# Cross-attention on one core: half-tile scores in two PSUM banks, a five-bank ring, and two of four mask copies moved from VectorE to transfers

## The reference

```python
qp = (q @ Wq.T + bq).reshape(b, t_q, h, d // h).transpose(0, 2, 1, 3)   # q = layernorm(x)
kp = (k @ Wk.T + bk)...; vp = (v @ Wv.T + bv)...                        # k = v = ctx_1024
scores = jnp.einsum('bhqd,bhkd->bhqk', qp, kp) / jnp.sqrt(jnp.float32(d))
scores = jnp.where((attention_mask == 1)[:, None], -jnp.inf, scores)
attn = jax.nn.softmax(scores, axis=-1)
out = jnp.einsum('bhqk,bhkd->bhqd', attn, vp)                           # x = x + out
```

## Time and profile before

| | |
|---|---|
| Median of 3 runs | 2255.85 us (2254.08 to 2257.64) |
| The profiled execution, its span | 2242.05 us, 2240.1 us |
| First stage | 31 periods, about 120 to 1557 us of the span |
| PE, DVE, ACT, POOL busy | 83%, 71%, 47%, 57% of the span |
| DMA engines' share in the periods | 0.50 |

### The profile page before, as it was taken

How to read it: one execution, slowest core, us unless ns; L and a number is a source line. 1 busy time by engine, 2 the same in 40 slices (tenths; PEclk the granted TensorE clock), 3 DMA queues, 4 the chain that set the end, 5 groups by cost and what they waited for, 6 DMA issues and landing times. The chain is left out here.

```text
span 2240.1 us, 62734 instructions
## 1 busy us (share of the span) xinstructions
PE 1865.6 (83%) x24523; PEld 1272.5 (57%) x24523; DVE 1583.0 (71%) x3092; ACT 1053.8 (47%) x1399; POOL 1284.5 (57%) x618
## 2 busy tenths in 40 slices
PE   2688888889888898888988888888778787499996
PEld 1255555555555565555655555565335566388885
DVE  3588787778777787877877777788667776544442
ACT  2255555556555565555655555554354442133332
POOL 3356767667776677766777657675345432144442
PEclk9699999999999999999999999999785655699998
DMA  3445544455444554445544455443253324377774
GB/s 107 117 98 134 112 104 106 102 122 122 104 105 105 135 107 104 104 102 125 120 102 107 101 129 115 99 107 65 85 207 105 130 79 145 122 213 225 238 218 133
DMA packets 172384, 277.73 MB, mean 124 GB/s; under 512 B 66676, under 2 KB 140212, under 8 KB 171843
## 3 DMA queue, kind: packets, MB, share of 16 engines
q1 hardware_dynamic: 163300, 261.77, 45.9%
q0 software_dynamic: 8832, 12.06, 2.8%
HBM read 163.02 MB, written 31.98 MB: 87 GB/s over the span
## 5 line engine op out<-in xcount | busy, mean ns | idle before, releaser
L451 DVE CUSTOM_DVE_ANT_0 junk<-ring,mbias 128x898 bf16<-128x898 f32 (+1 forms) x512 | 523.6, 1023 | 208.6 <-issue 206.7
L361 POOL TENSOR_TENSOR p_sum<-p_sum,pT 128x1024 f32<-128x1024 f32 x256 | 657.1, 2567 | 12.5 <-ACT pT L571 0.6
L571 ACT ACTIVATE pT<-score,lift 128x1024 f32<-128x1024 f32 (+1 forms) x416 | 456.9, 1111 | 66.7 <-PE score L678 58.0
L342 POOL TENSOR_TENSOR cp<-cx,cp 128x768 f16<-128x768 f32 (+1 forms) x128 | 277.9, 2172 | 120.0 <-ACT cp L530 120.0
L644 PE MATMUL ring<-wvp,cp 128*128 128x256 f16 (+1 forms) x2496 | 317.0, 277 | 9.2 <-DVE mx L451 8.2
L578 ACT ACTIVATE v<-ring 128x512 f32<-128x512 f32 (+1 forms) x224 | 126.9, 566 | 413.5 <-PE ring L644 411.4
L358 POOL TENSOR_TENSOR p_sum<-pT 128x1024 f32<-128x1024 f32 x32 | 75.5, 2359 | 388.5 <-ACT pT L571 388.5
L678 PE MATMUL score<-qst,kst 128*128 128x64 f16 x6656 | 271.8, 196 | 17.0 <-issue 11.3
L678 PEld LDWEIGHTS score<-qst,kst 128*128 128x128 f16 x6656 | 239.3, 101 | 81.4 <-issue 48.0
L479 DVE COPY kst<-mbias 64x6144 f16<-64x6144 f16 (+1 forms) x128 | 280.6, 2192 | 4.0
L644 PEld LDWEIGHTS ring<-wvp,cp 128*128 128x128 f16 (+1 forms) x2496 | 231.3, 100 | 77.4 <-issue 29.4
(11 more groups left out here) (222 smaller groups left out, 2474.1 us busy)
## 6 DMA issues: line engine op xcount, KB each, us to landing
cx<-in_ctxT SPq DMA_DIRECT2D x32, 1601.0 KB, 7.4
w1p<-wsp SPq DMA_DIRECT2D x23, 1408.0 KB, 8.5
kst<-kh SPq DMA_DIRECT2D x512, 52.1 KB, 2.3
msk<-in_mask SPq DMA_DIRECT2D x64, 400.2 KB, 9.3
kst<-kh SPq DMA_DIRECT2D x512, 48.0 KB, 2.2
wsp<-w_parts SPq DMA_DIRECT2D x24, 704.0 KB, 3.7
w2p<-wsp SPq DMA_DIRECT2D x23, 640.0 KB
kst<-kl SPq DMA_DIRECT2D x256, 52.1 KB, 2.3
```

What stands on the lines that cost most here:

```text
L342: pool.tensor_tensor(cp[:, j, 1, :, chunk(n)], cx[:, :, chunk(n)], cp[:, j, 0, :, chunk(n)], ALU.subtract).then_inc(cl_ready, 1)
L361: pool.tensor_tensor(p_sum[:], p_sum[:], pT[:, u], ALU.add).then_inc(added, 1)
L451: dve.tensor_tensor_reduce(junk[:, n % 2, :, 0:MPAIR[half]], ring[:, 0:2, 0:MPAIR[half]], mbias[:, j, MS[2 * half]:MS[2 * half] + 2 * MPAI ...
L571: act.activation(pT[0:n, u], scored, ACT.Exp, bias=lift[0:n, 0:1], scale=SSCALE).then_inc(exp_done, 1)
```

## The change

Scores. A step S or E is now half a tile (8 of 16 heads, one bank), so there are 26 of each in a block; `scored` has 2 banks, and step s waits for E(s-2). The ring has 5 banks; a maxima unit takes banks 0 and 1 or 2 and 3 in turn, and T takes ring banks 0 and 1. The order of the units within a half changes (TURNS).

Shift. SH has two operations (a maximum, then a clip of 128x8), and SPR, the copy of 1x1024 out of PSUM, moves from DVE to ACT.

Mask. Copies 0 and 3 are transfers from SP now, from `mbias` to `kst`, 1024 rows each (64 partitions x 16 heads; 768 and 898 bytes). Copies 1 and 2 stay on DVE, each with its own semaphore.

Orders. All five strings are new. On SP the order goes from CX QS ST0 QR ST1 to MD3 QR CX QS MD0 ST0 ST1. On POOL the four CL come after all A. The rest of the kernel is as it was.

```diff
-PE_ORDER = steps("K0 S0 K1 K2 O S1 M0 K3 S2 M1 S3 K4 M2 W0 M3 W1 W2 S4 M4 K5 S5 W3 M5 S6 K6 M6 S7 S8 W4 M7 K7 M8 W5 W6 M9 S9 W7 S10 M10 "
-                 "V0 W8 M11 V1 W9 M12 V2 S11 M13 S12 V3 M14 W10 W11 M15 V4 W12 V5 T V6")
-POOL_ORDER = steps("A2 CL0 A3 A4 A5 QB A6 A7 CL1 A8 CL2 A9 A10 CL3")
-DVE_ORDER = steps("N MA3 KL0 KL1 KL2 R X0 KL3 X1 X2 KL4 X3 MA0 X4 KL5 X5 X6 KL6 X7 X8 KL7 X9 X10 MP X11 X12 X13 X14 MA2 X15 SH MA1 SPR")
-SP_ORDER = steps("CX QS ST0 QR ST1")
+PE_ORDER = steps("S0 K0 S1 K1 S2 K2 O S3 S4 M0 K3 S5 K4 M1 S6 S7 W0 W1 S8 M2 M3 S9 K5 M4 S10 W2 W3 S11 M5 S12 K6 S13 S14 W4 W5 S15 M6 M7  "
+                 "S16 K7 W6 S17 S18 M8 M9 V0 S19 S20 M10 W7 W8 W9 M11 S21 S22 V1 S23 S24 W10 M12 M13 S25 V2 W11 M14 M15 W12 V3 V4 T V5  "
+                 "V6")
+ACT_ORDER = steps("E0 KH0 E1 KH1 E2 E3 E4 KH2 E5 KH3 E6 KH4 E7 E8 E9 E10 KH5 E11 E12 KH6 E13 E14 E15 E16 KH7 CH0 E17 E18 E19 E20 VH0 CH1  "
+                  "E21 E22 VH1 E23 E24 E25 VH2 CH2 CH3 VH3 VH4 SPR VH5 VH6")
+POOL_ORDER = steps("QB A2 A3 A4 A5 A6 A7 A8 A9 A10 CL0 CL1 CL2 CL3")
+DVE_ORDER = steps("N KL0 KL1 R X0 KL2 X1 KL3 KL4 X2 X3 X4 KL5 X5 KL6 X6 X7 KL7 X8 X9 X10 X11 MA2 X12 X13 X14 X15 SH MP MA1")
+SP_ORDER = steps("MD3 QR CX QS MD0 ST0 ST1")
...
+            scored = c1.enter_context(nc.psum_tensor("scored", [P, 2, 512], F32))
+            ring = c1.enter_context(nc.psum_tensor("key_ring", [P, 5, 512], F32))
...
+                    def lay_mask(b, j, c):
+
+                        after(sp, st_done, HT * b + (2 * GT * (c + 1) - HT if c < KC - 1 else 0))
+                        if c == 0 and not has_later(b - 1):
+                            sp.wait_ge(mask_ready, 2 * b + 2)
+                        sp.dma_start(kst[MASK_AT:P, :, chunk(c)],
+                                     mbias[MASK_AT:P, j, MS[c]:MS[c] + KWIDTH[c]].bitcast(F16).unsqueeze(1).to_broadcast([S, H, KWIDTH[c]])).then_inc(laid[c], 16)
...
-                        dve.tensor_reduce(m8[:], mx[:], AX.X, ALU.max).then_inc(m8_done, 1)
+                        dve.tensor_reduce(top_m[:], mx[:], AX.X, ALU.max).then_inc(m_all, 1)
+                        dve.wait_ge(m_all, b + 1)
+                        dve.tensor_scalar(m8[:], top_m[:], MOST_SHIFT * SHIFT, -MOST_SHIFT * SHIFT, ALU.min, ALU.max).then_inc(m8_done, 1)
...
-                        after(pe, exp_done, b * KT + (kt - 1))
-                        for h in range(H):
+                        after(pe, exp_done, b * HT + (step - 1))
+                        for h in range(PAIRS * half, PAIRS * half + PAIRS):
...
+                        act.activation(pT[0:n, u, HALF * half:HALF * half + HALF], scored[0:n, half, :], ACT.Exp, bias=lift[0:n, 0:1],
+                                       scale=SSCALE).then_inc(exp_done, 1)
```

More of the change, by code:

```diff
@@ L271, in chunk, with unit @@
                 return slice(KS[n], KS[n] + KWIDTH[n])
+            def unit(n):
+                half, at = divmod(n, PAIRS)
+                return half, at // 4, TURNS[at % 4]
             def strip(r, c):
@@ L470, in prepare_mask @@
                         after(dve, m_read, MUNITS * (b - 1))
-                        after(dve, laid, KC * (b - 1))
+                        for c in (0, KC - 1):
+                            after(dve, laid[c], 16 * (b - 1))
                         dve.tensor_scalar(mbias[:, j, 0:MS[2] + KWIDTH[2]], msk[:, 0:KS[3]], 1, -MASKED, ALU.is_equal, ALU.mult).then_inc(mask_ready, 1)
@@ L494, in period @@
                                 shift(nb)
[L495 to L499, removed]
+                            elif kind == "MA" and do_b:
                                 lay_mask(nb, nj, n)
@@ L559, in keep_kh, with exponentiate, spread_shift @@
                         act.activation(kh[:, t, chunk(c)], ring[:, BANK["K", k], 0:KWIDTH[c]], ACT.Identity, bias=bks[:, c % 2, t:t + 1]).then_inc(kh_kept, 1)
[L561 to L571, removed]
+                    def exponentiate(b, j, step):
+                        kt, half = divmod(step, 2)
+                        n, u = KROWS[kt], (KT * j + kt) % SLOTS
+                        act.wait_ge(st_done, b * HT + (step + 1))
+                        if half == 0:
+                            held = weights_before(j, kt)
+                            after(act, pv_done, b * KT + (held + 1))
+                            if held % KT in SUMMED:
+                                after(act, added, b * ADDS + (max(SUMMED.index(held % KT), 1) - (ADDS if held < 0 else 0)))
+                        act.activation(pT[0:n, u, HALF * half:HALF * half + HALF], scored[0:n, half, :], ACT.Exp, bias=lift[0:n, 0:1],
+                                       scale=SSCALE).then_inc(exp_done, 1)
+                    def spread_shift(b, j):
+                        act.wait_ge(mt_done, b + 1)
+                        at = BANK["T", 0]
+                        act.activation(qst[0:1, j].rearrange("o h q -> o (h q)"), ring[0:1, at:at + 2].rearrange("o s k -> o (s k)"),
+                                       ACT.Copy).then_inc(qaug_ready, 1)
                     def keep_v(b, j, u):
@@ L590, in period @@
                                 high_context(b + 2, j, n)
+                            elif kind == "SPR" and do_b:
+                                spread_shift(b + 1, 1 - j)
                     periods(act, period)
@@ L624, in ring_free @@
                                 after(pe, v_kept, (b - lap) * VU + at + 1)
+                            elif held == "T":
+                                after(pe, qaug_ready, (b - lap) + 1)
                     def project_k(b, j, k):
```

85 lines of the change are left out of this document (47 added, 38 removed), and 3 rows, old and new, of the table BANK.

## The result

The changed kernel took 2393.45 us (median of 4 runs, 2390.50 to 2396.63), the kernel before 2256.74 us beside it: ratio 1.0607, 95% interval 1.0588 to 1.0626. It is 6.1% slower. The forecast was 2327 us, slower, with a range of 2215 to 2410: right sign, and 66 us too low.

What follows compares the result with a forecast made beforehand. SP's queue was to bound: 40.8 + 1.0 (MD3) + 0.5 (MD0) + 6.8 (hold) = 49.1, taken as 49.0 us a period for 46.7; over 31 steps +71 us, so 2255.85 + 71 = 2327 us, range 2215 to 2410.

Steps and rivals of the forecast that it cites:

- SP becomes the bound, at 40.8 plus what is added: SP's queue: 40.8 us of issuing a period before; with the mask transfers and a hold, 49.0 us, never waiting for scores.
- rivals with no hold: SP's queue: SBUF-to-SBUF rows are not counted, so nothing is held; period 42.7 us, 2132 us; chance 0.18.
- with a short hold: SP's queue: limit just over 1856 open packets, part of cx and msk suffices; period 45.5 to 47.3 us; chance 0.12.
- with a price by packet: Mask transfers cost 0.128 us a packet; cx and msk end later, period 52.4 us, 2432 us; chance 0.06.
- MD3 with what it holds up, 1.0 us: SP's queue: issue of mask transfer MD3 plus the delay of transfers behind it, 1.0 us a period, bounds 0 and 1.6.
- my bounds of 1150 to 1856 open packets: SP's queue: SP stands still at somewhere between 1150 and 1856 packets issued but not yet moved.
- term that decides: What stands in front of MD0 on SP: unmoved transfers keep ST0 from being issued, a hold of 6.8 us.
- MD0's hold, 6.8 us: SP's queue: ST0's first transfer, behind MD0, is held 6.8 us a period until cx and msk have moved; chance 0.64.
- the c = 12.2: SP's queue: cx and msk have moved, and ST0's first issue ends, 12.2 us after CX's issue.
- The price of a row, 0.075 us: DMA: each of MD3's rows of 898 bytes takes 0.075 us, scaled by bytes from ST0's; 4.8 us in all.
- The extra of half tiles on ACT: ACT: 26 half exponentials at 598 ns instead of 13 at 1113 add 1.1 us a period, covered.
- The queue takes it all: SP's queue: mask transfers cause no hold; period 42.7 us, 2132 us, and 2105 to 2175 with issue and PE's waits; chance 0.18.

Runs made afterwards that it cites:

- e1: The changed kernel with all four mask copies on DVE (MA3 after X2, MA0 after X8), no mask transfers on SP: 2242.37 us, ratio 0.9911.
- e3: The changed kernel with both mask transfers writing one head (64 rows) instead of 16 (1024 rows) after block 0: 2169.2 us in one run.
- e9: The changed kernel with both mask transfers keeping 1,024 rows, but of 64 bytes instead of 768 or 898, after the first step: 2264.37 us in one run.
- e5: The changed kernel with MD0 moved behind ST0's transfers and ahead of ST1's on SP: 2372.3 us, ratio 1.0497.
- e8: The changed kernel without the mask copies of chunks 0 and 3 after the first step, by any engine: 2145.03 us, ratio 0.9496.
- e11: The changed kernel with all four mask copies on DVE, chunk 3's (MA3) right behind the normalization N: 2181.16 us, ratio 0.9660.
- e4: The changed kernel with the two mask transfers issued from ACT's queue (MD3 before E0, MD0 after E8) instead of SP's: 2321.18 us, ratio 1.0282.

## Why the prediction was right, and where it was off

**SP becomes the bound, at 40.8 plus what is added: right.** The kernel got slower, as forecast, but by 137 us and not by 71. Its issues fill 51.3 of 51.5 us, its wait for scores is gone, and e1 and e3 show that the rows of the mask transfers are the cause. The rivals with no hold (2132 us), with a short hold (2219 to 2275 us) and with a price by packet (2432 us) fell.

**MD3 with what it holds up, 1.0 us: the step that failed.** It is 0.65 + 4.3 = 5.0 us. I scaled the excess of one neighbour at the start by rows, and applied my bounds of 1150 to 1856 open packets to MD0 only; by them MD3, with 1024 rows, could hold nobody. It held QR and CX. The count contradicts the bound: by 806.30, when QR's second issue ended, MD3's 1024 rows were issued and 487 packets had moved, by 809.04, at CX's end, 903:

```profile
DMA packets 487, 0.44 MB, mean 125 GB/s; under 512 B 16, under 2 KB 487, under 8 KB 487
...
DMA packets 903, 0.81 MB, mean 130 GB/s; under 512 B 16, under 2 KB 903, under 8 KB 903
```

With QR's 128 rows and then CX's 256, some 700 and some 550 were open. Yet QS, three transfers of 256 rows, went out in 2.42 us (2.14 before) behind cx and msk, with some 1100 open at its end. One limit on the number of open packets, as I had it, doesn't describe both; what the limit counts stays open. The bounds were the prediction's "term that decides", so that MD0's hold came out near is in part luck.

**MD0's hold, 6.8 us: right in kind, 4.8 in size.** It ends when cx and nearly all of msk have moved, as predicted (818.73 here; e9 shows that MD0's own bytes don't matter for it). From CX's issue at 806.56 to the end of ST0's first issue at 818.73 it is 12.2 us, which is the c = 12.2 that I had worked out. But MD0's issue ended at c = 7.5, not 4.8, since MD3 held CX and then the loads as well; so 4.7 were left of the hold. What I had wrong is that cx and msk are needed for it: in e5, with ST0 between them and MD0, the stacking still takes 3.7 us more than before. Of the two holds together I had 7.8 us, and 9.8 were measured: MD3's was 4.0 short and MD0's 2.0 too long, and the second error hides half of the first.

**The price of a row, 0.075 us: too low.** MD3's rows took about 0.092 us each (window 803:809.5: 131 GB/s at share 0.82, so 131 / 0.82 / 16 = 10 GB/s an engine, 898 bytes in 0.090 us), MD0's 0.072 to 0.077. MD3's rows moved from 803.3 to 810.5, 7.2 us with QR's among them, for the 5.2 I gave the two. It landed in 8.8 us at the median, MD0 in 12.7:

```profile
kst<-mbias SPq DMA_DIRECT2D x32, 898.0 KB, 8.8
kst<-mbias SPq DMA_DIRECT2D x32, 768.0 KB, 12.7
```

The estimate from the Trainium skill (DMA: Bandwidth & Descriptors, Anatomy of one DMA), 2.1 us for MD3's bytes, is under a third of what the trace shows; that section's formula is for transfers issued by GpSimd, and this one is SP's. The Trainium skill (DMA: Bandwidth & Descriptors, Why small descriptors are slow) says that transfers between SBUF and SBUF don't suffer the penalty of small descriptors. Here they moved 131 GB/s where the long rows of cx and msk, from HBM, moved 313. But the stacking's rows of 1536 bytes, SBUF to SBUF too, took 0.128 us each, 12 GB/s an engine against MD3's 10, so length explains little of the distance; no run separates it from the place of the data.

**The sum.** Predicted 40.8 + 1.0 + 0.5 + 6.8 = 49.1; measured 40.8 + 5.0 + 0.65 + 4.8 = 51.3. With the 49.0 and 46.7 that I multiplied and the 51.5 and 46.4 that the SHs give, the miss is 31 x 2.5 = +77 and 31 x 0.3 = +9. Against it, the start saved 9 us and the end nothing, where I had +4 and -4 (-9), and the profiled execution (2391.89) lies 2 us under its median and not 14 (-12). 77 + 9 - 9 - 12 = 65 of the 66 us.

**PE and ACT.** PE's waits on maxima went, and ACT's on keys (KH4) came, 6.4 us a period for some 8 predicted. The extra of half tiles on ACT was under-sized: an exponential of 512 columns takes 684 ns, not 598, so 26 x 0.684 - 13 x 1.113 = +3.3 us a period, not +1.1. SP hid it here; it may be where e8's first wait of PE, for exponentials, comes from; no run tested it (40.1 us in 1170).

```profile
L596 ACT ACTIVATE pT<-scored,lift 128x512 f32<-128x512 f32 (+1 forms) x717 | 470.4, 684 | 204.7 <-PE scored L715 191.5
```

**"The queue takes it all", 42.7 us a period and 2132 us: even without a hold too low.** The nearest kernel, e3, has 44.2 and 2169.

## What to carry to other kernels

Where an issuing queue is as full as the bound, count a transfer of many short rows by what it does to those behind it: two of 1024 rows cost 1.3 us to issue and 9.1 us in their neighbours. Look where large transfers in flight and a many-row transfer meet in the queue, and move work to a queue only if its slack is there at that moment, which one gap in order of time shows and busy shares don't. A copy that an engine must make anyway belongs into its idle place, and there into one where GpSimd is idle too: moving MA3 by a few steps was worth 2.5% (ratios 0.9911 and 0.9660), cutting MA0 into quarters lost 0.8%.

## What the hardware showed that I had not expected

- The same VectorE copy, 64 x 6144, takes 1757 ns alone and, beside GpSimd, up to 3459 in e8 and 3927 in e1. In e8 one took 3.33 us, and GpSimd's product of 128x256, 0.67 us at the median in the kernel before, 2.18 beside it:

```profile
811.76 3.33 DVE L508 COPY kst<-mbias 64x6144 f16<-64x6144 f16 x1
813.45 2.18 POOL L377 TENSOR_TENSOR qh<-qh_all,sel_q 128x256 f16<-128x256 f16 x1
```

  They look as if one waits for the other and not as if they shared. The Trainium skill (SBUF — State Buffer, SBUF: two separate sides) says that they do: GpSimd and those VectorE instructions that use the pair of ports they have in common take it under an exclusive lock, for the whole instruction. That this is the cause here, no run isolated. It makes the removal of a copy worth more or less than its mean, by place (MA3: 2.77 us in e1, 2.04 in e11).
- The clip of 128x8 numbers has a median of 1.05 us and a maximum of 1.93 (minimum 0.17). No run told why.

```profile
L492 DVE TENSOR_SCALAR m<-top_m x32: 171/1050/1933, 110.9 to 1707.2; 128x8 bf16<-128x8 f32 x32
```

- With many rows under way PE can stand at the loop's start for up to 7.7 us with no semaphore to wait for (e4); it was 2.5 at most before. The page of the profile counts 3.87 MB of transfers of the kind "instruction" in e4. That PE's instructions, if they come this way, were late would explain the wait; this was not tested.
